# Releasing the branch later in the Sinkhorn alternation, and mixing 44 of 64 units on TensorE

## The reference, cut to what matters

```
x_norm = x * rsqrt(mean(x*x) + eps)
H_res  = sinkhorn_log((x_norm @ W_res.T).reshape(B, T, 4, 4) + H_res_base)   # 50 iterations, tau 0.1
H_pre  = softmax(x_norm @ W_pre.T + H_pre_base)          # 4 numbers a token
H_post = softmax(x_norm @ W_post.T + H_post_base)        # 4 numbers a token
H_res  = (1 - g) * I + g * H_res                         # g = sigmoid(gate)
x_pre  = einsum('btnc,btn->btc', x_streams, H_pre)       # 4 streams of 256
y      = x_pre @ W_branch
out    = einsum('btij,btjc->btic', H_res, x_streams) + einsum('btc,btn->btnc', y, H_post)
```

## Time and profile before

| | us |
|---|---|
| median of three executions | 1144.7 |
| the profiled execution | 1145.13 |
| its span, first to last instruction | 1143.3 |
| TensorE busy | 1074.3 (94%) |
| VectorE busy | 805.7 (70%) |
| ScalarE busy | 474.9 (42%) |
| mean granted clock of TensorE | 0.983 |

### The profile page before, as it was taken

The page is one execution under the profiler, slowest core; times in us unless marked ns, Lnnn a source line. Parts: engine busy times, 40 slices in busy tenths (PEclk is TensorE's granted clock), DMA queues, the critical chain, the costliest instruction groups (busy, mean ns, idle before and its releaser), DMA issues.

```text
span 1143.3 us, 17710 instructions
## 1 busy us (share of the span) xinstructions
PE 1074.3 (94%) x6412; PEld 902.8 (79%) x6412; DVE 805.7 (70%) x1837; ACT 474.9 (42%) x991; POOL 155.6 (14%) x162
## 2 busy tenths in 40 slices
PE   5999999999999998999999999999999999989636
PEld 3888888888888887888888878888888878877525
DVE  6754446576678868767668877666628799846998
ACT  4523324354544455545454454434214343422315
POOL 0000000333232232323323220000001000000000
PEclk9999999999999999999999999999999999999778
DMA  9876757234443323243444312699935413000001
GB/s 239 186 167 140 157 125 167 60 92 97 106 109 69 73 69 72 64 98 91 95 106 110 69 38 52 142 218 247 204 70 100 79 20 63 2 14 1 1 1 74
DMA packets 163947, 111.12 MB, mean 97 GB/s; under 512 B 73240, under 2 KB 155800, under 8 KB 163888
## 3 DMA queue, kind: packets, MB, share of 16 engines
q1 hardware_dynamic: 161632, 109.24, 43.7%
q10 hardware_dynamic: 2256, 1.11, 0.4%
HBM read 90.91 MB, written 18.87 MB: 96 GB/s over the span
## 4 chain that ended last, share of the span: by engine, by line
PE 82%; DVE 14%; ACT 2%; issue 1%; DMA 1%; ACTq 0%; POOL 0%; DVEq 0%
PE ps L480 28%; PE ps L537 28%; PE ps L875 8%; PE ps L466 5%; PE ps L548 4%; PE ps L565 3%; DVE wt L1411 2%; DVE small L1951 1%; DVE small L1955 1%; DVE small L1943 1%; DVE small L1947 1%; PE ps L654 1%; DVE small L1939 1%; DVE small L1935 1%; DMA raw<-in_L_xattn_q_proj_w 1%
## 5 line engine op out<-in xcount | busy, mean ns | idle before, releaser
L537 PE MATMUL ps<-wt,act 128*128 128x512 f32 x1536 | 389.2, 396 | 0.0
L480 PE MATMUL ps<-wt,act 128*128 128x512 f32 x1440 | 330.2, 391 | 4.5 <-DVE wt L1411 4.5
L480 PEld LDWEIGHTS ps<-wt,act 128*128 128x128 f32 x1440 | 271.3, 189 | 61.3 <-DVE act L1395 4.8
L537 PEld LDWEIGHTS ps<-wt,act 128*128 128x128 f32 x1536 | 275.9, 188 | 49.4
L1411 DVE TENSOR_TENSOR wt<-raw,wt 128x512 fp32r<-128x512 f32 x192 | 120.0, 684 | 85.7 <-ACT wt L992 85.7
L992 ACT ACTIVATE wt<-raw 128x512 fp32r<-128x512 f32 x192 | 106.5, 624 | 95.9 <-PE ps L480 52.5
L1395 DVE TENSOR_TENSOR act<-ps,act 128x512 fp32r<-128x512 f32 x112 | 75.9, 683 | 78.3 <-ACT act L987 78.3
L1403 DVE STREAM_TRANSPOSE raw<-raw 128x1024 f32<-128x1024 f32 x92 | 108.0, 1218 | 31.6 <-DMA raw<-in_L_xattn_o_proj_w 20.1
L875 PE MATMUL ps<-wt,act 128*128 128x512 f32 x480 | 122.8, 404 | 1.9 <-issue 1.2
L987 ACT ACTIVATE act<-ps 128x512 fp32r<-128x512 f32 x112 | 66.0, 597 | 114.0 <-PE ps L466 113.7
L2102 POOL TENSOR_TENSOR small<-small 128x4 f32<-128x4 f32 (+2 forms) x64 | 70.9, 1110 | 282.8 <-DVE small L1425 213.0
(11 more groups left out here) (149 smaller groups left out, 1086.0 us busy)
## 6 DMA issues: line engine op xcount, KB each, us to landing
xr<-in_ctx SPq DMA_DIRECT2D x64, 256.0 KB, 5.8
raw<-in_L_xattn_o_proj_w SPq DMA_DIRECT2D x32, 512.0 KB, 13.9
raw<-in_L_xattn_q_proj_w SPq DMA_DIRECT2D x28, 512.0 KB, 9.1
q_rows<-G SPq DMA_DIRECT2D x64, 128.0 KB, 3.5
xr<-q_rows SPq DMA_DIRECT2D x16, 512.0 KB
ot_hi<-spare SPq DMA_DIRECT2D x64, 128.0 KB, 3.0
act<-ot_hi SPq DMA_DIRECT2D x32, 256.0 KB, 9.1
raw<-in_L_xattn_k_proj_w SPq DMA_DIRECT2D x8, 512.0 KB, 9.7
```

Source lines behind the costliest of these rows:

```text
L480: mm = pe.matmul(banks[t], lhs(p == 2, c, t), wt[:, n_slot, int(p == 1), c, :], start=(acc_from and q == 0), stop=(acc_to and q == 3 * NC ...
L537: mm = pe.matmul(bank, src[int(p == 2)][:, c, kt * P:(kt + 1) * P], wt[:, slot, int(p == 1), c, :], start=(q == 0), stop=(q == 3 * NC - 1))
```

## The change

- The three instructions that release the branch move from after round 1 to after round 16 of the alternation.
- TensorE also mixes the third piece of tile 2, whose base stays in PSUM (bank 5, first 256 columns), so it has 16 + 16 + 12 = 44 units. ScalarE makes twelve diagonals for tile 2 instead of eight, and copies that piece out itself (`mixed(2, 1)`).
- VectorE keeps piece 3 of tile 2 and all of tile 3: 20 units, in four rounds of three and four rounds of two.
- Tile 3's bases are no longer split between bank 5 and the late banks. Both halves go through `late_base`, one after the other: TensorE writes the second half, ScalarE copies it, TensorE writes the first half over it, ScalarE copies it.
- The stores: first half of tile 2, first half of tile 3, second half of tile 2 (after TensorE's piece and VectorE's piece), second half of tile 3.

```diff
-        open_banks = [(ps[:, 0, :], ps[:, 1, :]), (ps[:, 2, :], ps[:, 3, :]), (ps[:, 4, :],), (ps[:, 5, :],)]
+        open_banks = [(ps[:, 0, :], ps[:, 1, :]), (ps[:, 2, :], ps[:, 3, :]), (ps[:, 4, :], ps[:, 5, 0:CW])]
...
-                                           (2, 1, out_ready, 1), (3, 0, out_ready, 2), (3, 1, out_ready, 3)):
+                                           (3, 0, out_ready, 2), (2, 1, mix_out, 6), (3, 1, out_ready, 3)):
...
-                for half in range(2 if t < 2 else 1):
+                def add_branch(part, i, stop):
+                    return pe.matmul(part, dmix[t % 2][:, 4 + i, :], yb, start=False, stop=stop)
+
+                for half in range((2, 2, 2, 0)[t]):
                     bank = open_banks[t][half]
-                    pe.matmul(bank, ident[:], xr[:, t, half * UW:(half + 1) * UW], start=True, stop=False)
+                    width = bank.shape[-1]
+                    pe.matmul(bank, ident[:], xr[:, t, half * UW:half * UW + width], start=True, stop=False)
                     if half == 0:
                         pe.wait_ge(y_read, t + 1)
...
-                if t >= 2:
-                    if t == 3:
-                        pe.wait_ge(base_added, 1)
-                    for i in (2, 3):
-                        pe.matmul(late_base[:, i - 2, :], ident[:], xr[:, t, i * CW:(i + 1) * CW], start=True, stop=False)
-                        mm = pe.matmul(late_base[:, i - 2, :], dmix[t % 2][:, 4 + i, :], yb, start=False, stop=True)
+                    for k in range(width // CW):
+                        mm = add_branch(bank[:, k * CW:(k + 1) * CW], 2 * half + k, False)
+
+                def late(half, pieces):
+                    for i in pieces:
+                        part = late_base[:, i % 2, :]
+                        pe.matmul(part, ident[:], xr[:, t, i * CW:(i + 1) * CW], start=True, stop=False)
+                        mm = add_branch(part, i, True)
+                    return mm
+
+                if t == 2:
+                    mm = late(1, (3,))
+                if t == 3:
+                    pe.wait_ge(base_added, 1)
+                    pe.wait_ge(y_read, 4)
+                    late(1, (2, 3)).then_inc(base_done, 1)
+                    pe.wait_ge(base_added, 2)
+                    mm = late(0, (0, 1))
                 mm.then_inc(base_done, 1)
...
-                if t >= 2:
-                    sc.wait_ge(base_done, t + 1)
-                    sc.activation(xr[:, t, UW:E].rearrange("p (i n) -> p i n", i=2), late_base, ACT.Copy
-                                  ).then_inc(base_added, 1)
+                if t == 2:
+                    sc.wait_ge(base_done, 3)
+                    sc.activation(xr[:, t, 3 * CW:E], late_base[:, 1, :], ACT.Copy).then_inc(base_added, 1)
                 if t == 3:
-                    sc.activation(xr[:, t, 0:UW], open_banks[t][0], ACT.Copy).then_inc(base_added, 1)
+                    for n, half in enumerate((1, 0)):
+                        sc.wait_ge(base_done, 4 + n)
+                        sc.activation(xr[:, t, half * UW:(half + 1) * UW].rearrange("p (i n) -> p i n", i=2), late_base,
+                                      ACT.Copy).then_inc(base_added, 1)
...
-                for n in range(16 if t < 2 else 8):
+                for n in range(16 if t < 2 else 12):
...
-                k = 2 * t + half if t < 2 else 2 + t
-                sc.wait_ge(mix_done, k + 1)
-                sc.activation(xr[:, t, half * UW:(half + 1) * UW], open_banks[t][half], ACT.Copy).then_inc(mix_out, 1)
+                sc.wait_ge(mix_done, 2 * t + half + 1)
+                if (t, half) == (2, 1):
+                    sc.wait_ge(out_ready, 1)
+                bank = open_banks[t][half]
+                sc.activation(xr[:, t, half * UW:half * UW + bank.shape[-1]], bank, ACT.Copy).then_inc(mix_out, 1)
...
             mixed(2, 0)
+            mixed(2, 1)
...
-                if k == 1:
+                if k == 16:
                     v.wait_ge(h8_out, 1)
...
-            mix(((2, 1), (3, 0)))
-            mix(((3, 1),))
+            mix(((2, 3), (3, 0), (3, 1)), ((2, 3), (3, 1)))
+            mix(((3, 2), (3, 3)), ((3, 3),))
```

More of the change, by code:

```diff
@@ L840, in base @@
                 pe.wait_ge(lg_read, 4)
-                for half in range(2 if t < 2 else 1):
+                def add_branch(part, i, stop):
+                    return pe.matmul(part, dmix[t % 2][:, 4 + i, :], yb, start=False, stop=stop)
+                for half in range((2, 2, 2, 0)[t]):
                     bank = open_banks[t][half]
-                    pe.matmul(bank, ident[:], xr[:, t, half * UW:(half + 1) * UW], start=True, stop=False)
+                    width = bank.shape[-1]
+                    pe.matmul(bank, ident[:], xr[:, t, half * UW:half * UW + width], start=True, stop=False)
                     if half == 0:
                         pe.wait_ge(y_read, t + 1)
-                    for i in (2 * half, 2 * half + 1):
-                        mm = pe.matmul(bank[:, (i % 2) * CW:(i % 2 + 1) * CW], dmix[t % 2][:, 4 + i, :], yb,
-                                       start=False, stop=(t == 3 and i == 1))
-                if t >= 2:
-                    if t == 3:
-                        pe.wait_ge(base_added, 1)
-                    for i in (2, 3):
-                        pe.matmul(late_base[:, i - 2, :], ident[:], xr[:, t, i * CW:(i + 1) * CW], start=True, stop=False)
-                        mm = pe.matmul(late_base[:, i - 2, :], dmix[t % 2][:, 4 + i, :], yb, start=False, stop=True)
+                    for k in range(width // CW):
[14 more added lines that the diff above has]
+                    mm = late(0, (0, 1))
                 mm.then_inc(base_done, 1)
@@ L860, in mix @@
                 for half, bank in enumerate(open_banks[t]):
-                    for i in (2 * half, 2 * half + 1):
+                    pieces = range(2 * half, 2 * half + bank.shape[-1] // CW)
+                    for i in pieces:
                         for j in range(NSTR):
@@ L864, in mix @@
                             mm = pe.matmul(bank[:, (i % 2) * CW:(i % 2 + 1) * CW], dres[t % 2][:, 4 * i + j, :],
-                                           z[:, t, j * CW:(j + 1) * CW], start=False, stop=(i % 2 == 1 and j == NSTR - 1))
+                                           z[:, t, j * CW:(j + 1) * CW], start=False, stop=(i == pieces[-1] and j == NSTR - 1))
                     mm.then_inc(mix_done, 1)
@@ L2075, in _, with mix @@
             settle()
-            def mix(pieces):
+            def mix(pieces, last):
                 for j in range(NSTR):
                     settle()
[L2081 to L2087, removed]
+                    for t, i in pieces:
+                        c = 16 * t + 4 * i + j
+                        o = xr[:, t, i * CW:(i + 1) * CW]
+                        done(v.scalar_tensor_tensor(o, z[:, t, j * CW:(j + 1) * CW], hres[:, c:c + 1], o,
+                                                    ALU.mult, ALU.add),
+                             out_ready if (t, i) in last and j == NSTR - 1 else dv)
             v.wait_ge(base_added, 3)
-            mix(((2, 1), (3, 0)))
-            mix(((3, 1),))
+            mix(((2, 3), (3, 0), (3, 1)), ((2, 3), (3, 1)))
+            mix(((3, 2), (3, 3)), ((3, 3),))
         @block.gpsimd
```

## The result

The changed kernel takes 1147.32 us (median of 19 executions, 1145.48 to 1149.97), the kernel before 1144.7 (19, 1142.81 to 1147.01): a ratio of 1.002, 95% interval 1.0012 to 1.0027, so 1.4 to 3.1 us slower. The forecast was 1146.9 us, 2.2 us slower.

What follows compares the result with a forecast made beforehand. Two nearly level sides, ScalarE's last copy and VectorE, were taken to bound the end. Late diagonals, longer mix and stores gave span 1146.05 against 1143.3, 2.75 us slower; less 0.5 for before's lucky cold stretch, 2.2: 1146.9 us, range 1143.8 to 1149.0.

Steps and rivals of the forecast that it cites:

- The release and VectorE: Alternation on VectorE: release 21.4 us later, chains 0 and 1 end as before; VectorE's mix 8.9 us against 10.53.
- The cover is used up: Branch on ScalarE, moved 21.4 us against a 17.41 us wait, ends after chain 0; diagonals of H_res start 4.3 us late.
- tile 3 cold: Summed case: TensorE's clock still falls in the 2.8 us gap ahead of tile 3's x_pre; forecast range's chance 0.5.
- tile 3 warm: Rival: tile 3's x_pre keeps TensorE's full clock, branch 1.7 us shorter, end 1.0 us above before's; chance 0.2.
- the first tile's branch: Branch start on TensorE: cold first x_pre and product lose 2.1 us to the clock, half a microsecond less than before.
- Tile 3's serial bases: Two base halves in series on TensorE and ScalarE: 1.0 us more, 0.8 net of tile 2's smaller copy.
- The mix: TensorE's mix starts warm at 2.4 GHz after a gap of about 1.1 us; 88 records take 19.2 us.
- The stores: Last four stores: ScalarE's last copy ends at 1143.1, second half of tile 2 follows, span ends at 1146.05 us.
- Which side ends last: Kernel's end: before, ScalarE's copy and VectorE nearly level; after, TensorE's mix and ScalarE's copy last, VectorE 1.6 us earlier.
- the traced cold stretch lucky: Before's mix: traced 3.0 us cold stretch below the 4.1 us mean, so before would lose 0.5 us more.
- The colder rival: Mix starts cold or branch's first stretch is longer: 0.5 to 1.5 us added, 4 us over before, 1148.8; chance 0.2.
- the rival in which VectorE sets the end: Branch done before chain 0, mix warm from 1119.2, VectorE's 1.6 us gained: 1143.1 us; chance 0.1.

Runs made afterwards that it cites:

- 40 units: Kernel before with only its release moved to after round 16, TensorE keeping 40 units: ratios 1.0002 and, repeated, 1.0009.
- the warm clock alone: Kernel before plus 38 unread matmuls ahead of TensorE's mix, release after round 1, 40 units: 1143.87 against 1145.48 us, ratio 0.9985.
- its second trace: Changed kernel unaltered, timed again in a second series beside the kernel before: 1146.95 against 1145.74 us, ratio 1.0018.
- The bridged kernel: Changed kernel with release after round 1 and 38 unread matmuls between branch and mix: 1143.62 us (0.9990) and again 1143.15 us (0.9981) against before.

## Why the prediction was right

- *The release and VectorE.* Computed 21.4 us later and nothing on VectorE; measured 21.4 us, rounds unchanged, chain 1's end 11.3 us behind chain 0's as before (1129.17 and 1117.84). Right. VectorE's units: 8.9 computed, 8.95 measured.
- *The cover is used up.* Computed: diagonals 4.3 us late with tile 3 cold, 2.6 with tile 3 warm. Measured: 4.82 and 2.67. The cold case was 0.5 us later: some 0.3 is the serial bases (below), and the rest the first tile's branch, which lost 2.4 us to the clock where I took 2.1. With 44 units, that the release does it is shown by taking it back (1.0003) and by pushing it on (5.7 us later for four rounds). With 40 units the traces show the same lateness, but the times show little of it.
- *Tile 3's serial bases.* Computed 1.0 us (0.8 with tile 2's smaller copy). In the trace after, from the end of y's copy (1115.18) to the end of the second copy (1120.61) are 5.4 us; before, from 1097.19 to 1101.33, 4.1 us. That is 1.3 us, 0.3 more than computed: after a wait TensorE's first pair of records took 0.67 and 0.70 us instead of 0.59, and the first of the two pairs started 0.15 us behind ScalarE's end, the second 0.05. Its own price was not measured by an experiment.
- *The mix.* Computed 19.2 us warm; measured 19.26 in both traces of the changed kernel, clock 1.00. That a gap of 0.97 us doesn't let it fall held in all five traces with such a gap.
- *The stores.* Computed: 2.95 us from the last copy's end (1143.1) to the end of the span (1146.05); measured 3.14 us (1140.63 to 1143.77). The 1.8 us outside the span were taken as the same after; they are 2.1 in the mean, and no term of the prediction stands for that.
- *Which side ends last.* Right for after. For before the prediction let both be level and named the traced cold stretch lucky, with 0.5 us for it. That term was probably too small: the warm clock alone gives 0.7 to 2.7 us, of which the trace has 0.3. It would make before slower than I had it, and so the difference smaller than forecast. On the other side the changed kernel's cold case came out worse than summed: its second trace ends 28.1 us from chain 0's end, 3.5 over before's trace instead of 2.75. The two pull in opposite ways, and 2.6 us came of it where 2.2 was forecast, with 1.2 us between the medians of the second series. The likeness of 2.6 and 2.2 is partly luck.
- *Readings and sums that don't hold.* In the earlier trace rows VectorE's last four slices are 6, 9, 9 and 8 tenths, so it is at nine tenths in two of them; the chain of waits bears the argument without it. The colder rival's 1148.8 is more than its terms give: 1146.9 and at most 1.5 are 1148.4. And the rival in which VectorE sets the end leaves out the prediction's own 0.8 us for the bases: with them the branch takes 39.4 us, and without both cold stretches 35.1, so it could not have come under 34.6.

That rival needed the branch to take under 34.6 us; it took 37.3 with tile 3 warm, and no trace had both stretches warm. The bridged kernel comes near to what that rival described: a hidden branch, a warm mix and both sides level, 1.3 us under before in the trace.

## What to carry to other kernels

When work is moved later under a cover, subtract the shift from the wait that proves the cover (17.4 us here against 21.4) before asking what the move is good for; what is left over is lateness, and here it ate the warm clock that the move bought. If TensorE has to be warm at a certain instant, give it cheap matmuls up to there rather than move real work there: once the cover was used up, 5.6 us more of lateness cost 4.1 to 5.5. And where two sides end level, one trace doesn't tell which is last in the median: time a kernel in which one of them is relieved, and look at the mean clocks of the executions that weren't traced.

## What the runs showed of the hardware

A gap of 2.80 us ahead of tile 3's x_pre let TensorE's clock fall in some executions and not in others: x_pre took 3.67 us in one trace of the changed kernel and 2.05 in the other. Of the eight traces with such a gap of 2.80 us six had x_pre cold (3.41 to 3.68 us) and two warm (2.05). That cold stretches differ between executions of one kernel, which the prediction had from no trace, is shown by this. The cold stretch at a mix behind a gap lasted 3.0, 3.5 and 5.7 us in three traces.

In the trace of the kernel with the release after round 13 the last store landed 4.1 us after its issue, where the longest was 2.6 to 2.7 us in every other trace, and the span ended 25.2 us behind chain 0 instead of some 23.3. Its DMA queues from 1138 to the end (packets, MB, share of the engines) hold a load of instructions beside the stores' data, between 1139 and 1140:
```profile
q8 instruction: 1, 0.02, 1.6%
```
Six other traces with 44 units show such a load later than 1125 us, and in none of them does it fall on the last four stores: it comes earlier, or after the span's end. Where it comes after the end (after round 1, after round 12, and the second trace of the changed kernel) 1.9, 2.5 and 2.8 us lie outside the span, and in all other traces 1.8. That the load delays a store, or the end of the execution, is an inference; no run took it away. Why it comes where it does stays open.
